# SyncE's requests for x one slot later and behind low-rank inputs and weights; TensorE's register reads behind the first product

## The chip, the cores and the metric

The kernel runs on one core of a Trainium2 chip. The metric is the device time of one execution in microseconds (us). A core has TensorE (PE in the profile, with PEld for its weight loads), VectorE (DVE), ScalarE (ACT), GpSimd (POOL) and SyncE (SP), which here only issues DMAs. Each engine works through its own list of instructions in order; semaphores order them against each other, and an instruction that waits holds all that stands behind it on its engine.

## The reference

The input x has 16 batches of 512 tokens with 512 features. Each batch has its own low-rank factors and condition. `gelu` is exact, the router picks 4 of 16 experts, each with 128 hidden units.

```python
z1 = einsum('bfi,bir->bfr', x, v[:, 0]) / 512
z = einsum('bfr,bor->bfo', z1, u[:, 0]) / 16
c = gelu(einsum('bfi,oi->bfo', x, W) + fc_bias + z + cond)
prob = softmax(c @ w_router + b_router)
mask = the 4 largest of 16 per token
h = relu(einsum('nd,ebd->neb', c, w1b) + b1b)
y = einsum('neb,ebd,ne->nd', h, w2b, mask) + b2
out = x + y
```

## The kernel before

Work runs in slots `s` = 0 to 99, written out by hand in the same order on every engine. In slots 0 to 63 (`SLOTS`) each slot does one piece of 128 tokens of the first layer: batch `b` = s // 4, quarter `q` = s % 4. TensorE's `layer(s)` makes it from a high and a low part of x and W (three products in place of one of full precision), with the low-rank term as one product more; `lowrank_in(b)` (q = 0) makes the factors. ScalarE applies `gelu`, TensorE transposes the result (`turn_batch`) and multiplies it with the router weights (`router`); per batch VectorE chooses experts (`logits`, `choose`, `choose_rest`, `place`) between small products of TensorE (`turn_logits` at the end of a slot with q = 1, `ranks` at q = 2, `counts` at q = 3, `positions` at q = 0). GpSimd's `place_rows(b, q)`, seven slots behind the layer, scatters each row to the lists of its four experts in HBM (`xg`), four indirect DMAs a slot, and `place_tiles` writes the table of tiles (`table`).

From slot 28 (`LAG`) on an expert tile of up to 512 rows is worked on in each slot, j = s - 28, 72 tiles (`NTILE`), so from 28 to 63 both kinds of work are interleaved. In slot s TensorE turns tile j + 1 (`turn_tile`, L1294: two quarters at the slot's start, two later), makes the hidden layer of tile j (`ffn1`, L1310 and L1315) and the result of tile j - 1 (`ffn2`, L1341). ScalarE and VectorE split what TensorE turned into high and low parts (`take_tile`), split the first and second weights of the tile's expert, and copy results out; GpSimd's `send` scatters them to `yt`, four indirect DMAs a slot. From tile 49 on a tile is two halves of 256 rows with an expert each. From tile 48 on (`PRE`) TensorE picks the second weights itself by a register that it loads from the tile's table row (`tabi`, L1289, inside `turn_tile` behind the wait for the tile, two registers for two experts). The last stage, from about 1430 us, sums the four results of each token with x and b2.

SyncE asks for all that comes from HBM, in the order of its own slots. `load_x(s)` (L331) reads a piece of 128 tokens into `stx`, 256 KB, and from piece 6 on waits first for VectorE's split of piece s - 2 (`v_xl` >= s - 1), since two buffers alternate. VectorE and ScalarE split piece s + 4 in slot s (`split_x`). `load_u(b + 1)` and `load_v(b + 2)` (q = 2) read the low-rank factors (`fu`, `fv`); `load_u` waits also for `turn_logits` of the batch before, since the logits share its buffer. Slots 2 to 17 read one expert's weights each (`w1f`, `w2f`, 256 KB each), slots 28 and on, every third, a padding of `xg` (L419). `load_tile(j + 2)` (L371 to L391) waits for the table, for the scattered rows that the tile may hold (L379), for TensorE's turn of tile j (L385), VectorE's ids of it (L386) and its split of the first weights of tile j (L387), and then asks for the rows (L389, 1056 KB) and the table row (L391). TensorE's `turn_tile` of tile j + 2 in slot s + 1 waits for both.

Of the kernel before, what the change touches and what calls it, by code (L numbers as in the profile page):

```python
# [9 lines left out]
NE = 16  # L10
# [7 lines left out]
NTILE = FULL + (HALVES + 1) // 2  # L18
SLOTS = 4 * NB
LAG = 28  # L20
# [10 lines left out]
PRE = 48  # L31
# [26 lines left out]
def chunks(j):  # L58

    return 2 if j == NTILE - 1 and HALVES % 2 == 1 else 4  # L60


def experts(j):

    return 1 if j < FULL else chunks(j) // 2


def x_buffer(s):

    return s if s < 4 else s % 2  # L70
# [53 lines left out]
def home(j):  # L124

    return 0 if j % 2 == 0 else 1 if j < HOME else 2
# [56 lines left out]
def rows_in(j):  # L183

    return sum(16 * (experts(i) + 1) for i in range(j % 2, j + 1, 2))


def per_half(j):

    return sum(experts(i) for i in range(j + 1))  # L190


def adaln_ffn(nc, xT, xrow, fvT, fuT, cond, fc, wT, wrT, br, w1T, b1T, w2T, b2R, outT):
    with ExitStack() as ctx:
        def sb(name, shape, dt):
            return ctx.enter_context(nc.sbuf_tensor(name, shape, dt))
# [56 lines left out]
        tabi = sb("tabi", [P, 2, 2, 4], I32)  # L253
# [73 lines left out]
        def _(sp):  # L327
            def load_x(s):
                if s >= 4:
                    sp.wait_ge(v_xl, s - 3 if s < 6 else s - 1)  # L330
                sp.dma_start(stx[:, x_buffer(s), :], xT[s]).then_inc(s_x[x_buffer(s)], 16)  # L331

            def load_v(b):
                if b > 0:
                    sp.wait_ge(v_v, b)
                sp.dma_start(fv[:, :, :], fvT[b]).then_inc(s_fv, 16)

            def load_u(b):
                if b > 0:
                    sp.wait_ge(v_u, b)  # L340
                if b > 1:
                    sp.wait_ge(p_lt, b - 1)
                sp.dma_start(fu[0:ZP, :], fuT[b]).then_inc(s_fu, 16)
                sp.dma_start(fu[ZP:ZB, :], gbd[b:b + 1, :].broadcast_to([2, D])).then_inc(s_fu, 16)
# [17 lines left out]
            r = [sp.alloc_register(f"r_sp{n}") for n in range(4)]  # L362
# [31 lines left out]
            def load_sum(i):  # L394
                n = len(xin)
                if i >= n:
                    sp.wait_ge(v_sum, 2 * (i - n) + 2)
                sp.dma_start(xin[i % n], xrow[i * SUM:(i + 1) * SUM, :].rearrange(
                    "(p h) d -> p h d", p=P)).then_inc(s_xr[i % n], 16)
# [5 lines left out]
            for s in range(LAG + NTILE):  # L405
                b, q = divmod(s, 4)
                j = s - LAG
                if s + 6 < SLOTS:
                    load_x(s + 6)
                if q == 2 and b + 1 < NB:  # L410
                    load_u(b + 1)
                if q == 2 and b + 2 < NB:
                    load_v(b + 2)
                if 2 <= s < 2 + NE:
                    sp.dma_start(w1f[:, s - 2, :], w1T[s - 2]).then_inc(s_ws, 16)
                    sp.dma_start(w2f[:, s - 2, :], w2T[s - 2]).then_inc(s_ws, 16)
                if LAG <= s < LAG + 3 * NE and (s - LAG) % 3 == 0:
                    e = (s - LAG) // 3
                    sp.dma_start(xg[e * LREG:e * LREG + HALF, :],  # L419
                                 xrow.rearrange("r d -> (r d)")[0:HALF * W].rearrange("(r d) -> r d", d=W)  # L420
                                 ).then_inc(s_pad, 16)
                if 0 <= j + 2 < NTILE:
                    load_tile(j + 2)
                if s == SLOTS + 16:
                    sp.wait_ge(p_tn, TURN_BATCH[SLOTS - 1] + 1)
                    sp.wait_ge(v_ix, NB)
                    sp.wait_ge(v_p2, NE)
                    sp.wait_ge(v_w2, PRE)
                    sp.wait_ge(p_lt, NB)
                    sp.wait_ge(v_u, NB)  # L430
                    sp.dma_start(b2f[:, :], b2R).then_inc(s_b2, 16)
                if SLOTS + 16 <= s < SLOTS + 16 + EARLY:
                    load_sum(s - SLOTS - 16)
# [744 lines left out]
        def _(pe):  # L1178
# [32 lines left out]
            def wait_taken(n):  # L1211

                if n >= 0 and TAKEN[n] is None:
                    pe.wait_ge(a_tn, n + 1)
                elif n >= 0:
                    pe.wait_ge(v_tn, TAKEN[n])
# [11 lines left out]
            def router(s):  # L1228

                b, half = divmod(s // 2, 2)  # L1230
                pe.wait_ge(a_tn, TURN_BATCH[s] + 1)
                if s == 1:
                    pe.wait_ge(s_br, 48)
                if b > 0:
                    pe.wait_ge(v_sv, b)
                if b > 0 and half == 1:
                    pe.wait_ge(v_tb, b)
                for k in range(KC):
                    last = pe.matmul(rps[2 * NE * k:2 * NE * (k + 1), half * 256:(half + 1) * 256], wrz[:, k, :],
                                     gs[:, k, :], start=True, stop=True)  # L1240
                last.then_inc(p_r, 1)
# [38 lines left out]
            r = [pe.alloc_register(f"r_pe{n}") for n in range(6)]  # L1280
            expert = {}

            def turn_tile(j, c):
                if c == 0:
                    pe.wait_ge(s_gr[j % 2], rows_in(j))
                    if j >= PRE:
                        expert[j] = []
                        for h in range(experts(j)):
                            pe.reg_load(r[2 * (j % 3) + h], tabi[0:1, j % 2, h, 0:1])  # L1289
                            expert[j].append(pe.snap(r[2 * (j % 3) + h], min_val=0, max_val=NE - 1))  # L1290
                n = TURN_TILE[j, c]
                wait_taken(n - 2)
                for k in range(KC):
                    last = pe.transpose(trn[n % 2][:, k * P:(k + 1) * P], grs[j][:, c, k * P:(k + 1) * P],  # L1294
                                        idf[:, :])
                last.then_inc(p_tn, 1)

            def ffn1(j):
                pe.wait_ge(v_w1, per_half(j))
                pe.wait_ge(a_tn, TURN_TILE[j, chunks(j) - 1] + 1)  # L1300
                if j > 0:
                    pe.wait_ge(a_hv, per_half(j - 1))
                pe.wait_ge(v_z, min((j + LAG - 1) // 4 + 1, NB))
                g = gsbs[home(j)]
                n = TILE if j < FULL else HALF
                parts = [slice(h * n, (h + 1) * n) for h in range(experts(j))]
                for h, cols in enumerate(parts):
                    for k in range(KC):
                        for a in (HI, LO):
                            pe.matmul(hid[:, cols], w1x[h][:, a, k * P:(k + 1) * P], g[:, k, HI, cols],  # L1310
                                      start=(h == 0 and k == 0 and a == HI), stop=False)
                pe.wait_ge(v_tn, TAKEN[TURN_TILE[j, chunks(j) - 1]])
                for h, cols in enumerate(parts):
                    for k in range(KC):
                        last = pe.matmul(hid[:, cols], w1x[h][:, HI, k * P:(k + 1) * P], g[:, k, LO, cols],  # L1315
                                         start=False, stop=(h == len(parts) - 1 and k == KC - 1))
                last.then_inc(p_f1, 1)
# [48 lines left out]
            for s in range(LAG - 1, SLOTS + 1):  # L1366
                b, q = divmod(s, 4)
                j = s - LAG
# [27 lines left out]
            for s in range(SLOTS + 1, LAG + NTILE + 1):  # L1396
                j = s - LAG
                if j + 1 < NTILE:
                    for c in range(2):
                        turn_tile(j + 1, c)  # L1400
                if s == SLOTS + 1:
                    router(SLOTS - 1)
                if s == SLOTS + 4:
                    positions(NB - 1)
                if s == SLOTS + 6:
                    positions(NB)
                if j < NTILE:
                    ffn1(j)
                if j + 1 < NTILE:
                    for c in range(2, chunks(j + 1)):  # L1410
                        turn_tile(j + 1, c)
                for c in range(chunks(j - 1)):
                    ffn2(j - 1, c)
                if s == SLOTS + 1:
                    turn_logits(NB - 1)
                if s == SLOTS + 2:
                    ranks(NB - 1)
                if s == SLOTS + 3:
                    counts(NB - 1)
# [36 lines left out]
```

## Time and profile before

| | us |
|---|---|
| median of 3 runs | 1648.52 |
| lowest and highest run | 1642.79, 1649.10 |
| the profiled execution | 1648.12 |
| its span, first to last instruction | 1646.3 |
| TensorE busy | 951.5 (58%) |
| VectorE busy | 837.2 (51%) |
| ScalarE busy | 583.9 (35%) |
| GpSimd busy | 576.1 (35%) |
| mean granted clock of TensorE | 0.785 |
| stages: first layer alone, interleaved, tiles alone, sum | 0 to 213, to 1054, to 1420, to 1646 |

The profile gives for each engine when it was busy and what ended its waits: the instruction or DMA whose semaphore update came last. A trailing q (SPq, PEldq) is an engine's sequencer, so a wait or an issue. "issue" is time for which no releaser is seen, "remote" a semaphore update that no recorded instruction matches. A wait is named by the instruction that follows it: "PE trn L1294 <- DMA tabi<-table" is TensorE idle ahead of the tile's first transpose until its table row, asked for last, has landed.

### The profile page before, as it was taken

What the parts mean: (1) busy time and instruction counts of PE and PEld (TensorE: products, weight loads), DVE (VectorE), ACT (ScalarE), POOL (GpSimd) and SP (SyncE); (2) the same over time, 40 slices, a digit from 0 to 9 for tenths busy, and PEclk for the clock granted to TensorE, in tenths of its full rate; (3) what the DMA queues carried; (4) which work ended last, traced back from release to release, by engine and by line L of the source; (5) the groups of instructions that cost most, each with busy time, mean ns of one, the idle gap of its engine ahead of it and who ended that gap; (6) DMA issues with size and microseconds to landing.
All of it is one profiled execution on the core that took longest, in us unless ns stands there. A gap on an engine that the chain in (4) does not pass through costs nothing.

```text
span 1646.3 us, 17908 instructions
## 1 busy us (share of the span) xinstructions
PE 951.5 (58%) x4924; PEld 765.4 (46%) x4924; DVE 837.2 (51%) x1966; ACT 583.9 (35%) x1063; POOL 576.1 (35%) x589
## 2 busy tenths in 40 slices
PE   8755656466556465565565479866888898400000
PEld 7543545355445354454354357654777777300000
DVE  4432333333334242343343346563786786698777
ACT  6332333233233242333333245552665566200000
POOL 0554431332333323243423426556444344400000
PEclk9977787787777777787777789987999999755555
DMA  5765443534543534434434557657668765799999
GB/s 188 257 236 188 147 162 121 177 126 147 170 143 143 170 107 166 162 135 159 167 120 153 176 185 249 237 210 257 223 223 271 263 209 204 273 419 427 425 430 395
DMA packets 103234, 354.82 MB, mean 216 GB/s; under 512 B 29961, under 2 KB 29961, under 8 KB 92384
## 3 DMA queue, kind: packets, MB, share of 16 engines
q1 hardware_dynamic: 59104, 217.21, 38.5%
q0 software_dynamic: 43936, 136.37, 21.2%
q8 instruction: 41, 0.67, 0.2%
q14 instruction: 57, 0.47, 0.1%
q10 hardware_dynamic: 96, 0.10, 0.0%
HBM read 200.47 MB, written 169.65 MB: 225 GB/s over the span
## 4 chain that ended last, share of the span: by engine, by line
PE 39%; DMA 26%; issue 11%; DVE 8%; another core or an unknown queue 6%; SPq 5%; ACT 4%; POOL 1%; ACTq 1%; DVEq 0%; POOLq 0%
DMA tabi<-table 15%; PE hid L1310 9%; PE trn L1294 8%; PE lay L1204 8%; DMA w2l<-yt 8%; PE yps L1341 5%; PE hid L1315 3%; DVE xs L813 2%; PE hid L1190 1%; DVE stx L1026 1%; PE trn L1224 1%; ACT xs L585 1%; DMA outT<-ys 1%; PE lay L1341 1%
## 5 line engine op out<-in xcount | busy, mean ns | idle before, releaser
L547 POOL DMA_INDIRECT yt<-ys,ids x238 | 256.0, 1076 | 450.0 <-ACT ys L690 332.0
L1294 PE MATMUL trn<-idf,gr 128*128 128x128 f32 x720 | 127.8, 334 | 354.8 <-DMA tabi<-table 327.5
L521 POOL DMA_INDIRECT xg<-grow,ix x224 | 219.5, 980 | 231.5 <-DVE ix L909 167.5
L1294 PEld LDWEIGHTS trn<-idf,gr 128*128 128x128 f32 x720 | 105.5, 173 | 373.7 <-DMA tabi<-table 335.6
L1204 PE MATMUL lay<-w2l,xs 128*128 128x512 f32 x768 | 199.6, 411 | 0.0
L1204 PEld LDWEIGHTS lay<-w2l,xs 128*128 128x128 f32 x768 | 147.9, 198 | 31.0
L633 ACT ACTIVATE gsb<-trn 128x512 fp32r<-128x512 f32 x144 | 81.0, 598 | 190.8 <-PE trn L1294 187.5
L844 DVE TENSOR_TENSOR above<-gr,tabi 128x12 f32<-128x12 int32 x45 | 7.6, 169 | 263.5 <-DMA tabi<-table 263.5
L633 ACT ACTIVATE xs<-trn 128x512 fp32r<-128x512 f32 x88 | 50.4, 597 | 211.5 <-PE trn L1294 160.5
L835 DVE TENSOR_TENSOR gsb<-trn,gsb 128x512 fp32r<-128x512 f32 x144 | 94.5, 686 | 55.4 <-ACT gsb L633 48.9
L663 ACT ACTIVATE hv<-hid,b1c 128x512 f32<-128x512 f32 (+1 forms) x94 | 52.7, 584 | 191.2 <-PE hid L1315 159.8
L1010 DVE COPY ys<-yps 128x512 f32<-128x512 f32 x97 | 66.8, 689 | 72.4 <-PE yps L1341 62.2
L813 DVE TENSOR_TENSOR xs<-stx,xs 128x512 fp32r<-128x512 f32 x64 | 44.1, 691 | 101.7 <-ACT xs L585 92.0
L1310 PE MATMUL hid<-gsb,w1c 128*128 128x512 f32 (+1 forms) x288 | 92.2, 478 | 1.7 <-DVE w2c L976 1.7
L835 DVE TENSOR_TENSOR xs<-trn,xs 128x512 fp32r<-128x512 f32 x88 | 58.6, 687 | 53.1 <-ACT xs L633 45.9
L1294 PE MATMUL trn<-idf,grow 128*128 128x128 f32 x424 | 60.6, 282 | 28.8 <-issue 10.8
L1310 PEld LDWEIGHTS hid<-gsb,w1c 128*128 128x128 f32 x288 | 65.9, 259 | 14.1 <-DVE w2c L976 2.4
L547 POOL DMA_INDIRECT yt<-stx,ids x48 | 49.4, 1029 | 56.6 <-ACT stx L690 43.7
L1341 PE MATMUL yps<-w2l 128*128 128x512 f32 x246 | 68.9, 418 | 0.0
L1294 PEld LDWEIGHTS trn<-idf,grow 128*128 128x128 f32 x424 | 47.3, 143 | 43.6 <-issue 26.6
L1310 PE MATMUL hid<-xs,w1c 128*128 128x512 f32 x176 | 67.0, 543 | 0.0
L612 ACT ACTIVATE grow<-lay 128x512 f32<-128x512 f32 x56 | 33.4, 597 | 90.8 <-PE lay L1209 55.4
(220 smaller groups left out, 2026.0 us busy)
## 6 DMA issues: line engine op xcount, KB each, us to landing
gr<-xg SPq DMA_DIRECT2D x45, 1056.0 KB
xs<-yt SPq DMA_DIRECT2D x16, 2048.0 KB, 19.8
w2l<-yt SPq DMA_DIRECT2D x15, 2048.0 KB, 20.2
grow<-xg SPq DMA_DIRECT2D x45, 528.0 KB
stx<-xT SPq DMA_DIRECT2D x64, 256.0 KB, 4.9
outT<-ys SPq DMA_DIRECT2D x31, 512.0 KB, 21.0
xg<-xrow SPq DMA_DIRECT2D x16, 528.0 KB
w2f<-xrow SPq DMA_DIRECT2D x16, 512.0 KB, 14.8
```

Source lines behind the costliest of these rows:

```text
L521: pool.indirect_dma_start(out=xg, out_offset=bass.IndirectOffsetOnAxis(ap=ix[:, row_buffer(b), q, k:k + 1], axis=0), in_=grows[row_buffer( ...
L547: pool.indirect_dma_start(out=yt, out_offset=bass.IndirectOffsetOnAxis(ap=ids[:, j % 8, c:c + 1], axis=0), in_=yss[result_buffer(j)][:, c, ...
L633: act.activation(gsbs[home(j)][:, :, HI, c * P:(c + 1) * P], trn[n % 2][:, :].rearrange("p (k t) -> p k t", k=KC), ACT.Copy).then_inc(a_tn, 1)
L663: act.activation(hv[:, h * n:(h + 1) * n], hid[:, h * n:(h + 1) * n], ACT.Relu, bias=b1c[:, bass.DynSlice(e[h], 1)]).then_inc(a_hv, 1)
L813: dve.tensor_tensor(xs[:, x_home(b), :, LO, cols], stx[:, x_buffer(s), :].rearrange("p (k t) -> p k t", k=KC), xs[:, x_home(b), :, HI, col ...
L835: dve.tensor_tensor(gsbs[home(j)][:, :, LO, c * P:(c + 1) * P], trn[n % 2][:, :].rearrange("p (k t) -> p k t", k=KC), gsbs[home(j)][:, :, ...
L1010: dve.tensor_copy(yss[result_buffer(j)][:, c, :], ypss[result_bank(j, c)][:, :]).then_inc(v_y, 1)
L1204: pe.matmul(lay[s % 2][:, :], xs[:, x_home(b), k, h, cols], wls[:, k, a, :], start=(k == 0 and a == HI and h == HI), stop=False)
L1294: last = pe.transpose(trn[n % 2][:, k * P:(k + 1) * P], grs[j][:, c, k * P:(k + 1) * P], idf[:, :])
L1310: pe.matmul(hid[:, cols], w1x[h][:, a, k * P:(k + 1) * P], g[:, k, HI, cols], start=(h == 0 and k == 0 and a == HI), stop=False)
L1315: last = pe.matmul(hid[:, cols], w1x[h][:, HI, k * P:(k + 1) * P], g[:, k, LO, cols], start=False, stop=(h == len(parts) - 1 and k == KC - 1))
L1341: last = pe.matmul(ypss[result_bank(j, c)][:, :], hx[:, c * P:(c + 1) * P], w[a], start=(i == 0), stop=(i == 2))
```

## The change

In a slot SyncE asks for x behind `load_u`, `load_v` and the weights. In slots 0 to 26 it is still piece s + 6; slot 27 asks for none; from slot 28 to 58 it is piece s + 5. `load_x` and its wait are as before, and so is the place of the padding and of `load_tile` behind it. TensorE's register reads leave `turn_tile` and stand behind `ffn1(j)`, for tile j + 1, without a wait of their own (the wait for the tile was passed at the slot's start).

```diff
             for s in range(LAG + NTILE):
                 b, q = divmod(s, 4)
                 j = s - LAG
-                if s + 6 < SLOTS:
-                    load_x(s + 6)
                 if q == 2 and b + 1 < NB:
                     load_u(b + 1)
...
                     sp.dma_start(w2f[:, s - 2, :], w2T[s - 2]).then_inc(s_ws, 16)
+                if s < LAG - 1:
+                    load_x(s + 6)
+                elif LAG <= s < SLOTS - 5:
+                    load_x(s + 5)
                 if LAG <= s < LAG + 3 * NE and (s - LAG) % 3 == 0:
...
             def turn_tile(j, c):
                 if c == 0:
                     pe.wait_ge(s_gr[j % 2], rows_in(j))
-                    if j >= PRE:
-                        expert[j] = []
-                        for h in range(experts(j)):
-                            pe.reg_load(r[2 * (j % 3) + h], tabi[0:1, j % 2, h, 0:1])
-                            expert[j].append(pe.snap(r[2 * (j % 3) + h], min_val=0, max_val=NE - 1))
...
+            def read_experts(j):
+
+                expert[j] = []
+                for h in range(experts(j)):
+                    pe.reg_load(r[2 * (j % 3) + h], tabi[0:1, j % 2, h, 0:1])
+                    expert[j].append(pe.snap(r[2 * (j % 3) + h], min_val=0, max_val=NE - 1))
...
                 if j < NTILE:
                     ffn1(j)
+                if PRE <= j + 1 < NTILE:
+                    read_experts(j + 1)
```

## Rows read from the trace of the kernel before

**Rows 1.** The page's fourth part: the chain that ended last, by line.

```profile
DMA tabi<-table 15%; PE hid L1310 9%; PE trn L1294 8%; PE lay L1204 8%; DMA w2l<-yt 8%; PE yps L1341 5%; PE hid L1315 3%; DVE xs L813 2%; PE hid L1190 1%; DVE stx L1026 1%; PE trn L1224 1%; ACT xs L585 1%; DMA outT<-ys 1%; PE lay L1341 1%
```

**Rows 2.** Windows: length; PE, PEld, DVE, ACT, POOL busy; clock, DMA share, GB/s.

```profile
42.00:206.00 164.00, 104.12 (x525) 77.50 (x525) 56.61 (x255) 52.65 (x91) 83.41 (x85) 0.80 0.59 207
...
213.00:985.00 772.00, 448.00 (x2102) 358.84 (x2102) 285.66 (x786) 258.46 (x461) 259.32 (x252) 0.76 0.44 151
985.00:1165.00 180.00, 136.11 (x685) 106.35 (x685) 102.57 (x297) 84.91 (x154) 101.31 (x101) 0.88 0.66 234
...
1157.00:1405.00 248.00, 214.62 (x1332) 184.01 (x1331) 184.12 (x401) 153.92 (x301) 113.44 (x110) 0.97 0.71 235
```

**Rows 3.** Waits, 213 to 985 us: us in total, times, longest.

```profile
PE trn L1294 <- DMA tabi<-table: 323.5, 31, 13.0
```

**Rows 4.** SyncE's own waits, 213 to 985 us.

```profile
SPq L331 <- DVE xs L813: 622.5, 29, 25.0
SPq L379 <- DMA xg<-grow,ix: 7.1, 1, 7.1
```

**Rows 5.** The chain that ended last, in order: start, us, what.

```profile
413.56 0.33 SPq L331
...
437.12 0.70 DVE xs L813
...
437.84 0.33 SPq L331
...
439.75 6.70 DMA tabi<-table
...
446.49 1.97 PE trn L1294 x8
```

**Rows 6.** The same chain later: its longest tile landing of the stage.

```profile
939.99 9.73 DMA tabi<-table
```

**Rows 7.** TensorE's timeline: starts of slots 27, 59 and 64.

```profile
213.51 1.97 PE L1294 MATMUL trn<-idf,gr 128*128 128x128 f32 x8 [0.62 <-issue]
...
985.22 1.32 PE L1294 MATMUL trn<-idf,gr 128*128 128x128 f32 x8
...
1053.73 1.04 PE L1294 MATMUL trn<-idf,gr 128*128 128x128 f32 x8
```

**Rows 8.** SyncE's timeline: table row requests of slots 59, 60 and 71.

```profile
981.46 0.43 SPq L391 DMA_DIRECT2D tabi<-table  x1
...
992.96 0.45 SPq L391 DMA_DIRECT2D tabi<-table  x1
...
1157.47 0.42 SPq L391 DMA_DIRECT2D tabi<-table  x1
```

**Rows 9.** Waits of the whole trace whose releaser is unknown.

```profile
DVE fu L863 <- remote: 53.3, 6, 12.0
...
ACT hv L663 <- remote: 26.3, 5, 9.5
```

**Rows 10.** SyncE's timeline in a slot with q = 2 and padding.

```profile
389.27 0.33 SPq L331 DMA_DIRECT2D stx<-xT  x1
...
390.88 0.57 SPq L419 DMA_DIRECT2D xg<-xrow  x1
...
394.18 0.43 SPq L391 DMA_DIRECT2D tabi<-table  x1
```

**Rows 11.** The page's sixth part: x, KB each, us to landing.

```profile
stx<-xT SPq DMA_DIRECT2D x64, 256.0 KB, 4.9
```

**Rows 12.** The chain at the start of slot 82.

```profile
1251.19 8.26 DMA tabi<-table
1259.45 0.92 issue
1260.37 1.94 PE trn L1294 x8
```

**Rows 13.** Waits, 1190 to 1417 us.

```profile
PE trn L1294 <- DMA tabi<-table: 9.9, 5, 2.8
```

## Prediction

> **What bounds the kernel now.** I read the chain that ended last first: 15% of the span is the landing of the tile DMAs, for which TensorE waits in `turn_tile` [rows 1]. The windows by stage show where [rows 2]. Between 213 and 985 us, while batches and expert tiles run interleaved, TensorE is busy 448 of 772 us at a granted clock of 0.76 (a mixture of the levels 1.2 and 2.4 GHz), the DMA engines carry 44%, GpSimd is busy 259 us. No engine is full. From 985 to 1165 us the clock is 0.88 and DMA 66%, from 1157 to 1405 us 0.97 and 71%. The waits of the slow stage: 31 waits of TensorE for the tile, 323.5 us, about 10 us in each slot [rows 3]. Then SyncE's own waits: 622.5 us in 29 waits stand at L331, the wait inside `load_x`, and behind it, of all that `load_tile` itself waits for, the largest is 7.1 us, once [rows 4].
>
> The chain through one slot tells why [rows 5]. VectorE splits piece s + 4 of x at 437.12; only then may SyncE ask for piece s + 6 (437.84), and behind that, in the same queue, for tile j + 2 (439.75). Its rows land 6.70 us later, TensorE starts the slot at 446.49, and the split of the next piece stands near the end of that slot's VectorE work. So each slot holds a closed loop: split, x request, tile request, landing, whole slot, split. From x request to x request (413.56 to 437.84) it is 24.3 us. A tile needs of this only what its own waits in `load_tile` say: tile j turned, its ids taken, its first weights split, all of the slot before, and the scattered rows.
>
> **The change part by part.**
>
> *x one slot later (slots 28 to 58).* SyncE now asks in slot s for piece s + 5, whose wait is for the split of piece s + 3, made in the slot before. No request is added or dropped (31 in this stage). The loop of rows 5 stays but spans two slots instead of one: with this landing 24.3 / 2 = 12.2 us a slot, and with the longest landing of the chain, 9.73 us [rows 6], (24.3 + 3.0) / 2 = 13.7 us. That is a floor, no longer the bound, if a slot's other work is as long.
>
> What a slot costs with the tiles there in time is shown by the trace itself: from slot 58 on SyncE has no x to ask for. TensorE starts slot 27 at 213.51, slot 59 at 985.22 and slot 64 at 1053.73 [rows 7]. So the 32 slots that are held take 771.7 us, 24.1 each; the five free slots with the same layer, turns, feed-forward and scatters take 68.5, 13.7 each. Over the twelve free slots by SyncE's tile requests (981.46 to 1157.47) it is 176.0 us, 14.67 each [rows 8]. These have less TensorE work towards their end, but they also hold stalls whose releaser the profile does not know: one of ScalarE's waits for the hidden layer is 9.5 us long, and VectorE's waits for the router product come to 53.3 us in six, up to 12.0 [rows 9]. The held slots have besides a split of x on ScalarE and VectorE and 256 KB of DMA that slots 60 to 63 lack; both engines are busy at most 57% of the free stage [rows 2], so I put no own term for it, and take the larger row, 14.67. 32 x 14.67 = 469; the saving is 771.7 - 469 = 302 us. Ends for this term: 12.2 a slot (390, saving 381) and 17.7 (below; 566, saving 205).
>
> *What the request is moved behind.* In every fourth slot `load_u` (two DMAs) and `load_v` (one) now come first, and `load_u` waits for TensorE's `turn_logits`, the last work of the slot before: the queue holds x and the tile behind it until then. In such a slot x, u, v and a third of the time the padding are issued from 389.27 to 390.88, and the tile's last request is at 394.18, 4.9 us behind the first one [rows 10]. From the slot's start: 4.9 + 6.7 = 11.6, with the long landing 14.6, against a free slot of 14.7. It fits, barely; if it misses, it costs up to 1 us in 8 slots, inside the rounding of the term above. An x piece lands after 4.9 us [rows 11] (seen where it could be timed) and is needed by ScalarE at the end of the next slot, some 20 us behind the request: no cost. In slots 2 to 17 the two weight requests go ahead of x. x still waits there for the same split of its own slot, which is later than the weights' issue, and is needed two slots on: 0, with -5 to +10 us as ends, since the early stage has DMA at 59% and stalls too [rows 2, 9]. The padding write (every third slot) stays ahead of the tile as before.
>
> *Registers (slots 75 to 98).* Before, TensorE's two loads stand between the landing of a tile and its first transpose: landing 8.26 us, then 0.92 us of issue, then the turn [rows 12]. Behind ffn1 they go beside matmuls that are queued already. Where the tile is late 0.92 us goes; where it is not, queued matmuls cover the loads today too. Five of TensorE's gaps there are put down to the tile [rows 13]; I take seven of the 24 slots, since the loads themselves hide a landing that is just late: 6 us. Ends: 24 x 0.92 = 22 us gained in every slot, or 22 us lost, if the second pair of turns starts later by the loads and nothing covers that. What is late next in those slots is the landing itself, through the split of the first weights.
>
> **Sum.** The profiled execution took 1648.1 us (span 1646.3 and 1.8 around it), the median of the runs is 1648.5, so no correction. 1648.1 - 302 - 6 = 1340 us. After slot 59 I leave all else as it is: the last stage of 216 us is not touched.
>
> **A rule against it.** GpSimd's instructions take 259.3 / 252 = 1.03 us each in the held stage and 101.3 / 101 = 1.00 us in the free one, where VectorE's busy share is 0.57 instead of 0.37 [rows 2]: denser VectorE work did not slow them. The Trainium skill ("SBUF — State Buffer", section "Who interferes with whom") says that the port pair shared by GpSimd and VectorE is an exclusive lock, so that one waits for the other's whole instruction, and with the change more of both overlap. By that rule the time would be the one of the last rival below; the trace so far does not agree.
>
> **Rivals.**
> - *The two-slot loop is the bound* and the free work is shorter than in slots 59 to 70, because more TensorE work runs at full clock: 12.2 a slot, 390 us, total 1648 - 381 - 6 = 1261 us. For it: one free slot is 11.5 us long by SyncE's requests (981.46 to 992.96 [rows 8]). Against: five of them together take 13.7 each.
> - *Late completions in each batch.* With GpSimd at 8 indirect DMAs a slot (10.6 us with gaps of 0.3) in a slot of 14, its streaks get longer, and each batch of four slots pays one stall of VectorE's longest, 12.0 us [rows 9]: 14.67 + 3.0 = 17.7 a slot, 566 us, total 1648 - 205 - 6 = 1437 us. For it: six such waits in 16 batches now, with GpSimd less busy for most of them. Against: the five free slots take 13.7 each with their stalls.
> - *The scatter's landing takes the place of x* in every fourth slot (7.1 us where it was seen once [rows 4]): 8 x 7.1 = 57 us, total 1397 us. Slots of two lengths would show it.
> - *Slower than before: a stall of that size in every slot*, in ScalarE's and VectorE's waits on TensorE, from the faster mixture of scatters, tile reads and x. 13.7 + 12.0 = 25.7 a slot, 822 us, total 1648 + 50 = 1698 us. It decides from 24.1 - 13.7 = 10.4 us a slot on. Six waits averaging 8.9 us in the whole trace are far from one in each slot.
> - *It does not do what it says*: another wait of `load_tile` is satisfied just as late as x's, and the start stays: 1648 us. Those waits are all for the slot before, so there is little for it.
> - *GpSimd becomes the bound*: if each of its instructions doubled, 8 x (2.06 + 0.30) = 18.9 a slot, 604 us, total 1648 - 168 - 6 = 1474 us. The rows of GpSimd speak against it.
>
> **How the numbers follow.** The forecast of 1340 (1295 to 1385) 0.57; the two-slot loop 0.14; late completions per batch 0.14; the scatter's landing 0.08; GpSimd as bound 0.02; does nothing 0.02; slower 0.03. The range runs from 1272, between forecast and the short rival (its outer half left out), to 1430, just short of the batch stalls; about 2 in 10 is left out. Less than 0.5%, 8 us, can't be told from no change here. Faster by more: all but two cases, 0.95; within: 0.02; slower: 0.03.
>
> **What would show it.** Right: SyncE's wait at L331's place falls from 622 us to under half, TensorE's wait for tabi from 323 to under 50, the start of slots 28 to 58 14 to 15 us apart, granted clock there above 0.9, DMA above 65%; in the last tile slots no 0.9 us of issue between landing and turn. Wrong: slots of 17 us and more with ScalarE's and VectorE's waits put down to no known releaser; a wait at `load_u` or for scattered rows in every fourth slot that TensorE then repeats; or an early stage longer than 206 us.

## The result and the profile after

The changed kernel takes 1355.8 us, median of 4 runs (1348.3 to 1366.9), beside 1645.7 us of the kernel before in its 4 runs (1641.3 to 1649.1): a ratio of 0.8245, with a 95% interval of 0.8171 to 0.8320. The forecast was 1340, the range 1272 to 1430. The profiled execution took 1362.6 us, its span is 1360.8.

The windows of the changed kernel, by stage. Columns as in [rows 2]. The bounds are the starts of TensorE's first transpose in slots 27, 59, 75 and 98 (98 is the last slot that turns a tile).

```profile
0.00:200.70 200.70, 148.07 (x754) 110.67 (x754) 78.77 (x330) 79.96 (x137) 88.82 (x116) 0.85 0.63 215
200.70:684.77 484.07, 412.62 (x2117) 323.35 (x2117) 281.61 (x789) 254.77 (x461) 254.01 (x253) 0.93 0.71 240
684.77:906.40 221.63, 169.75 (x808) 132.96 (x809) 126.25 (x342) 107.27 (x193) 116.48 (x116) 0.87 0.63 224
906.40:1119.00 212.60, 184.54 (x1173) 156.10 (x1172) 154.26 (x333) 128.88 (x257) 94.42 (x92) 0.99 0.70 231
1119.00:1360.80 241.80, 13.33 (x75) 10.53 (x73) 191.25 (x175) 8.70 (x18) 15.90 (x14) 0.54 0.96 399
```

The second row answers the interleaved row of [rows 2]: the same work (TensorE 2117 records, 2102 in the slightly shorter window before) in 484 instead of 774 us, the granted clock 0.93 instead of 0.76, DMA 71% instead of 44%. TensorE's busy time fell from 448 to 413 us although its work is the same, since more of it ran at the upper of the two levels, 2.4 GHz.

SyncE's own waits in this stage, 201 to 685 us (us in total, times, longest), answering [rows 4]:

```profile
SPq L331 <- DVE xs L815: 219.9, 18, 15.6
SPq L342 <- PE rps L1250: 77.7, 7, 12.0
SPq L379 <- DMA xg<-grow,ix: 1.7, 1, 1.7
```

And the waits of the other engines in the same window, the tile's row answering [rows 3] and the five largest without a known releaser answering [rows 9]:

```profile
ACT xs L635 <- remote: 36.0, 12, 5.0
ACT grow L614 <- remote: 29.8, 8, 4.9
ACT hv L665 <- remote: 19.0, 5, 6.0
DVE fu L865 <- remote: 18.1, 6, 4.4
DVE ys L1012 <- remote: 14.7, 4, 4.9
PE trn L1291 <- DMA tabi<-table: 13.9, 8, 3.5
```

The wait inside `load_x` went from 622 to 220 us, and TensorE's wait for the tile from 323.5 us in 31 waits to 13.9 in 8: the tile is there. SyncE now waits at L342 too, inside `load_u`. New in bulk are the waits put down to "remote", which the last two sections come back to.

To see where the time went in every kernel, I took the same four starts from each trace's TensorE timeline. A stage is the difference of two of them:

| span, us | to slot 27 | slots 27-58 (each) | 59-74 | 75-97 | rest | span |
|---|---|---|---|---|---|---|
| before | 211.4 | 773.8 (24.2) | 208.6 | 211.9 | 240.6 | 1646.3 |
| after | 200.7 | 484.1 (15.1) | 221.6 | 212.6 | 241.8 | 1360.8 |
| difference | -10.7 | -289.7 | +13.0 | +0.7 | +1.2 | -285.5 |

The first start of slot 27 before is at 211.44, one half-turn ahead of the row at 213.51 that [rows 7] has. The stage so far called 771.7 us is 773.8 by that.

### The profile page after: what moved, and what is told of

It is laid out like the page before. It is cut to its first block, busy times and chain, and to the rows that moved or that the text cites. A ratio compares the mean times of both kernels' runs of the same rounds, so it can differ in the third digit from the quotient of the medians.

```text
span 1360.8 us, 17932 instructions
## 1 busy us (share of the span) xinstructions
PE 928.3 (68%) x4924; PEld 733.6 (54%) x4924; DVE 832.1 (61%) x1966; ACT 579.6 (43%) x1063; POOL 569.6 (42%) x589
## 4 chain that ended last, share of the span: by engine, by line
PE 35%; DMA 18%; DVE 13%; issue 12%; another core or an unknown queue 9%; ACT 6%; POOL 3%; SPq 2%; ACTq 1%; DVEq 0%; POOLq 0%
DMA w2l<-yt 10%; PE hid L1314 7%; PE trn L1291 7%; PE lay L1206 6%; PE yps L1345 5%; DMA tabi<-table 5%; PE hid L1319 4%; PE hid L1192 2%; DVE stx L1028 2%; POOL xg L523 2%; DMA yt<-ys,ids 2%; DMA outT<-ys 1%; POOL yt L549 1%; PE lay L1345 1%
## 5 line engine op out<-in xcount | busy, mean ns | idle before, releaser
L549 POOL DMA_INDIRECT yt<-ys,ids x238 | 243.6, 1023 | 302.9 <-ACT ys L692 172.2
L523 POOL DMA_INDIRECT xg<-grow,ix x224 | 223.1, 996 | 150.3 <-DVE ix L911 86.3
L1206 PE MATMUL lay<-w2l,xs 128*128 128x512 f32 x768 | 204.7, 419 | 0.0
L1206 PEld LDWEIGHTS lay<-w2l,xs 128*128 128x128 f32 x768 | 152.1, 203 | 32.9
L1291 PE MATMUL trn<-idf,gr 128*128 128x128 f32 x720 | 109.8, 295 | 68.2 <-ACT stx L623 15.7
L1291 PEld LDWEIGHTS trn<-idf,gr 128*128 128x128 f32 x720 | 89.6, 152 | 86.7 <-issue 26.0
L1314 PE MATMUL hid<-gsb,w1c 128*128 128x512 f32 (+1 forms) x288 | 78.9, 424 | 2.9 <-DVE w2c L978 2.9
L1314 PEld LDWEIGHTS hid<-gsb,w1c 128*128 128x128 f32 x288 | 56.1, 222 | 13.6 <-DVE w2c L978 4.0
L1345 PE MATMUL yps<-w2c,hh 128*128 128x512 f32 x180 | 60.9, 420 | 1.6 <-ACT stx L692 1.6
L692 ACT ACTIVATE ys<-yps 128x512 f32<-128x512 f32 x97 | 57.8, 596 | 9.4 <-remote 4.7
```

The costliest lines, as they stand in the source:

```text
L523: pool.indirect_dma_start(out=xg, out_offset=bass.IndirectOffsetOnAxis(ap=ix[:, row_buffer(b), q, k:k + 1], axis=0), in_=grows[row_buffer( ...
L549: pool.indirect_dma_start(out=yt, out_offset=bass.IndirectOffsetOnAxis(ap=ids[:, j % 8, c:c + 1], axis=0), in_=yss[result_buffer(j)][:, c, ...
L692: act.activation(yss[result_buffer(j)][:, c, :], ypss[result_bank(j, c)][:, :], ACT.Copy).then_inc(a_y, 1)
L1206: pe.matmul(lay[s % 2][:, :], xs[:, x_home(b), k, h, cols], wls[:, k, a, :], start=(k == 0 and a == HI and h == HI), stop=False)
L1345: last = pe.matmul(ypss[result_bank(j, c)][:, :], hx[:, c * P:(c + 1) * P], w[a], start=(i == 0), stop=(i == 2))
```

## The experiments

They ran on three chips, in two groups of times, and this has to be known ahead of them. On chip 7 the kernel before took 1646.2 us (median of 7 runs, 1638.6 to 1653.2), as on the chip of the result above (1645.7), whose number is not on record. On chip 1 the same program took 1536.9 us (19 runs, 1527.3 to 1543.3), on chip 6 1536.8 (13 runs, 1527.7 to 1545.1). I write A for chip 7 and the chip of the result, and B for chips 1 and 6: the names stand for the two groups of times, not for two chips. The changed kernel itself ran on A alone. The four runs from x_only to order_only in the table are of chip 1, the four below them of chip 6. Ratios are always to the kernel before on the same chip; traces of the kernel before exist for A alone. In the columns, a slot of 27-58 is the mean of 32, and the others are whole stages.

| run | chip | median us | ratio, 95% interval | to slot 27 | slot 27-58 | 59-74 | 75-97 |
|---|---|---|---|---|---|---|---|
| changed_again | A | 1357.2 | 0.8233 (0.8176 to 0.8290) | 201.6 | 15.15 | 217.3 | 212.2 |
| tile_first | A | 1345.7 | 0.8187 (0.8161 to 0.8213) | 196.9 | 14.69 | 216.7 | 211.8 |
| x_behind_tile | A | 1351.9 | 0.8227 (0.8197 to 0.8256) | 197.6 | 14.96 | 220.0 | 212.1 |
| gpsimd_pauses | A | 1284.6 | 0.7798 (0.7766 to 0.7830) | 198.3 | 13.58 | 204.0 | 210.8 |
| x_only | B | 1186.2 | 0.7704 (0.7668 to 0.7741) | 149.1 | 13.19 | 175.0 | 202.4 |
| registers_only | B | 1530.0 | 0.9959 (0.9931 to 0.9987) | 149.3 | 24.26 | 171.9 | 195.9 |
| later_only | B | 1178.6 | 0.7658 (0.7630 to 0.7686) | 150.9 | 12.93 | 174.4 | 205.6 |
| order_only | B | 1532.3 | 0.9969 (0.9946 to 0.9992) | 147.8 | 24.04 | 173.9 | 202.1 |
| short_pauses | B | 1179.8 | 0.7697 (0.7652 to 0.7742) | 149.0 | 13.05 | 173.9 | 197.0 |
| pauses_everywhere | B | 1209.5 | 0.7875 (0.7829 to 0.7921) | 153.7 | 13.36 | 190.5 | 196.1 |
| pauses_tile_first | B | 1205.5 | 0.7858 (0.7815 to 0.7902) | 153.5 | 13.07 | 191.2 | 196.7 |
| before_with_pauses | B | 1535.1 | 0.9989 (0.9959 to 1.0020) | 146.1 | 23.77 | 182.0 | 203.3 |

**The two halves of the change: x_only and registers_only.** The first is the kernel before with only SyncE's part of the diff, the second with only TensorE's:

```diff
 x_only, SyncE
-                if s + 6 < SLOTS:
-                    load_x(s + 6)
...
+                if s < LAG - 1:
+                    load_x(s + 6)
+                elif LAG <= s < SLOTS - 5:
+                    load_x(s + 5)
 registers_only, TensorE
-                    if j >= PRE:
-                        expert[j] = []
...
+                if PRE <= j + 1 < NTILE:
+                    read_experts(j + 1)
```

> SyncE's part of the change alone; TensorE's register reads stay in the turn as in the kernel before. My theory: it carries all of the gain, and the register part nothing, since in the changed kernel's trace the gap of about 1 us has only moved from ahead of the turn to behind ffn1: within 5 us of the changed kernel's 1356 us. Rival (the registers brought the 6 us of the sum): 6 us more than the changed kernel.

> TensorE's part alone; SyncE as in the kernel before. My theory: within 3 us of the kernel before (1646 us), with slots 75 to 98 taking 211 to 213 us as in both kernels. Rival (0.92 us in seven slots): 6 us less than before. Rival (a bubble in each of 23 slots): up to 20 us more.

x_only has the large gain, registers_only leaves the held stage at 24.26 us a slot. What the register reads are worth shows in the last tile slots: 202.4 us with the reads in the turn, 195.9 with them behind `ffn1`. Both expectations held the registers for nothing; on B the rival, 6 us, came in (6.9 us between the two medians, ratio 0.9959, so the size is known to some 4 us). The chain that ended last in x_only, as [rows 12] of before, still has the gap between landing and turn; in registers_only it hasn't. Columns: start, us, what; first x_only, then registers_only.

```profile
839.87 7.86 DMA tabi<-table
847.73 0.93 issue
848.66 1.06 PE trn L1296 x8
```

```profile
1178.86 8.05 DMA tabi<-table
1186.91 0.04 issue
1186.96 1.08 PE trn L1289 x4
```

**Later or behind: later_only and order_only.** The change does two things to the request for x. Each alone, on the kernel before:

```diff
 later_only: at its old place, ahead of load_u
-                if s + 6 < SLOTS:
+                if s < LAG - 1:
                     load_x(s + 6)
+                elif LAG <= s < SLOTS - 5:
+                    load_x(s + 5)
 order_only: behind load_u, load_v and the weights
-                if s + 6 < SLOTS:
-                    load_x(s + 6)
...
+                if s + 6 < SLOTS:
+                    load_x(s + 6)
```

> Kernel before, but x is asked one slot later from slot 28 on and stays ahead of the low-rank inputs and weights in every slot. My theory: the loop over two slots is the whole effect, so slots 27 to 58 take about 15 us each, and only the early stage keeps its 211 us instead of 201 us: 1356 + 10 = 1366 us. Rival (the order counts as well in slots with q = 2): the load_u wait no longer holds x, 1350 us. Rival (the order carries the gain): near 1640 us.

> Kernel before, but each slot's x request (still piece s + 6) stands behind low-rank inputs and weights. My theory: x still waits for the split of its own slot, so slots 27 to 58 stay at 24 us each; the early stage gains 10 us because weights leave the queue earlier: 1636 us. Rival: the early 10 us are another effect or chance: 1646 us.

later_only keeps the whole gain (0.7658 beside x_only's 0.7704, intervals that overlap), order_only has a slot of 24.04 us and gains some 5 us in all (0.9969, an interval that nearly reaches 1); the 10 us that were expected of it in the early stage did not come (147.8 us beside 149.3 in registers_only). So the gain is that of the slot later, and the new place among the low-rank inputs has no part in it on B. The windows of both stages, later_only first:

```profile
150.90:564.80 413.90, 386.40 (x2117) 309.16 (x2117) 282.32 (x791) 257.20 (x465) 259.50 (x258) 0.97 0.83 284
```

```profile
147.80:917.20 769.40, 446.29 (x2117) 357.59 (x2117) 286.28 (x789) 259.11 (x462) 267.58 (x258) 0.77 0.45 154
```

**The change once more: changed_again.** No edit, on chip 7 beside the next three.

> The changed kernel itself, beside the experiments. The four kernels of the first group ran at 0.93 of the earlier time of the kernel before (1537 instead of 1646 us) and showed no late completion of TensorE at all, where the first traces show 70 and 178. My theory: that lateness depends on the chip and not on the kernel; where it is absent, x part and register part add up: 1186 - 6 = 1180 us, ratio 0.767. Where it is present: 1356 us, ratio 0.824. Rival: the register part is lost beside the x part: 1186 us.

1357.2 us and 15.15 us a slot: the first trace's 15.13 was no accident. The stages agree to 1 us each but for slots 59 to 74, 217.3 and 221.6, so a single trace's number there is good to about 4 us. The early stage is no better: four kernels with the same early slots have it at 196.9 to 201.6 us on A.

**The wait at load_u: tile_first.** In the changed kernel, from slot 28 on, the tile is asked for first, then u, v, x and the padding.

```diff
+                if 0 <= j + 2 < NTILE:
+                    load_tile(j + 2)
+                if q == 2 and s >= LAG and b + 1 < NB:
+                    load_u(b + 1)
+                if q == 2 and s >= LAG and b + 2 < NB:
+                    load_v(b + 2)
+                if LAG <= s < SLOTS - 5:
+                    load_x(s + 5)
...
-                if 0 <= j + 2 < NTILE:
-                    load_tile(j + 2)
```

It was made for this place in the changed kernel's chain, in a slot with q = 2 and padding (L342 is `load_u`'s wait for `turn_logits`):

```profile
482.73 1.90 PE rps L1250 x8
...
484.64 0.02 SPq L342
...
486.31 1.58 SPq L421
...
491.92 1.39 SPq L387
...
494.05 0.70 SPq L389
...
494.77 7.32 DMA tabi<-table
502.09 0.04 issue
502.13 1.39 PE trn L1291 x8
```

From L342 to the table's request SyncE needs 10.1 us (484.64 to 494.77), with u, v, x, the padding (1.58 us alone) and the steps of `load_tile` in one row, and the landing is 7.32 more: 17.5 us for a slot that should be 15. This is the longest of the eight such slots of the stage: from `load_u`'s first request to the tile's last the three with padding take 7.2, 10.1 and 9.5 us, the five without 3.4 to 4.7. In x_only on B the same rows take 4.4 to 4.6 and 3.4 to 3.6 us; why they are longer on A is open.

> Changed kernel, but from slot 28 on the tile request stands first in SyncE's slot, then u, v, x, padding; nothing of the x chain or of load_u's wait is left ahead of the tile. My theory: the two-slot loop and load_u's wait still cost the interleaved stage: TensorE's waits for the tile (20, 48 us in x_only) go, slots fall from 13.2 to the 12.0 us of the free slots, 30 to 38 us less than the changed kernel. Rival (those waits hide others, TensorE's own work and its partners are the bound): less than 8 us.

14.69 us a slot on A, 1345.7 beside 1357.2 us of the change: 11.5 us less, where 30 to 38 were expected and under 8 by the rival. In the traces the held stage is 14.6 us shorter, but so is the early stage by 4.7, which the edit leaves alone. The two ratios' intervals touch (0.8176 to 0.8290 and 0.8161 to 0.8213), so the sign is likely and the size is not settled.

**x not later but behind the tile: x_behind_tile.** The kernel before, with the request for piece s + 6 moved to the end of the slot.

```diff
-                if s + 6 < SLOTS:
-                    load_x(s + 6)
...
                 if 0 <= j + 2 < NTILE:
                     load_tile(j + 2)
+                if s + 6 < SLOTS:
+                    load_x(s + 6)
```

> Kernel before with one move: in each slot load_x(s + 6), which still waits for the split of its own slot, stands behind load_tile(j + 2) instead of ahead of everything. x is not asked later in slots. My theory: what counts is only which wait the tile stands behind; the tile now waits for the x chain of the slot before, as in later_only: ratio 0.766 (or 0.82 where completions are late). Rival (asking for x later is itself what helps, by less DMA traffic or a later split): near 1.0.

It asks for the same piece as the kernel before, in the same slot, and waits for the same split. It is not independent of later_only, though: from slot 28 on both kernels send SyncE's requests in the same order, tile j + 2, then piece s + 6, then the next slot's u, v, padding and tile j + 3; only the slot under which the program writes the piece differs. So it repeats later_only on A. SyncE's waits in the held stage, as [rows 4], of this run and then of later_only:

```profile
SPq L331 <- DVE xs L813: 292.2, 27, 14.2
SPq L379 <- DMA xg<-grow,ix: 2.5, 1, 2.5
```

```profile
SPq L331 <- DVE xs L815: 294.1, 31, 13.8
```

292 us of waiting at L331, more than in the changed kernel, and yet 14.96 us a slot and 1351.9 us in all; 294 us in later_only, which has the shortest slots of all, 12.93 us. How long SyncE waits for a split is no measure of the cost. What cost 290 us was that tile j + 2 stood behind piece s + 6 instead of ahead of it, and that piece waits for a split that is made only in the present slot.

**GpSimd's streaks: gpsimd_pauses.** The changed kernel, with five small memsets, each waiting for the one before, ahead of and behind the four scatters to `xg` in slots 31 to 66. They compute nothing that is used.

```diff
+            def pause():
+                for _ in range(5):
+                    if paused[0]:
+                        pool.wait_ge(g_p, paused[0])
+                    paused[0] += 1
+                    pool.memset(idle[:, :], 0.0).then_inc(g_p, 1)
...
                 if 0 <= s - 7 < SLOTS and not first:
+                    pause()
                     place_rows((s - 7) // 4, (s - 7) % 4)
+                    pause()
```

> Changed kernel, with GpSimd made to pause (five small chained memsets, an estimated 1 to 2 us) ahead of and behind the four scatters of a slot in slots 31 to 66, so that no more than six indirect DMAs stand back to back. My theory where completions are late: the lateness needs a streak of about eight, so it shrinks, and the kernel is 10 to 40 us faster than the changed one in spite of the pauses. Where they are not late: 0 to 25 us slower. Rival (the lateness comes from DMA traffic, not from GpSimd's streaks): it stays with the pauses.

1284.6 us: work was added to an engine, and 72.6 us went (1357.2 to 1284.6), on chip 7, where 10 to 40 were expected. GpSimd's timeline in one slot (start, us, engine, line, operation, then the idle time before it):

```profile
322.56 0.82 POOL L563 MEMSET idle<- 128x16 f32 x5
323.54 0.97 POOL L525 DMA_INDIRECT xg<-grow,ix  x1 [0.15 <-issue]
324.81 0.96 POOL L525 DMA_INDIRECT xg<-grow,ix  x1 [0.30 <-issue]
326.08 0.96 POOL L525 DMA_INDIRECT xg<-grow,ix  x1 [0.30 <-issue]
327.35 0.96 POOL L525 DMA_INDIRECT xg<-grow,ix  x1 [0.31 <-issue]
328.31 0.80 POOL L563 MEMSET idle<- 128x16 f32 x5
```

The window of the held stage, beside the changed kernel's second row above:

```profile
198.27:632.80 434.53, 392.49 (x2115) 312.48 (x2116) 281.19 (x789) 258.00 (x464) 285.31 (x524) 0.96 0.77 266
```

Against changed_again the held stage is 50.1 us shorter (484.7 to 434.6) and slots 59 to 74 are 13.3 us shorter. The stages that the edit leaves alone differ by 3.3 us (to slot 27) and 1.4 us (75 to 97). This kernel is the fastest of all that ran on A.

**What in the pause does it: short_pauses, pauses_everywhere, pauses_tile_first, before_with_pauses.** One memset in place of five; five behind every group of indirect DMAs in all slots; the same with the order of tile_first; and the pauses of gpsimd_pauses in the kernel before.

```diff
 short_pauses
-                for _ in range(5):
+                for _ in range(1):
 pauses_everywhere
                 if 0 <= s - 7 < SLOTS and first:
                     place_rows((s - 7) // 4, (s - 7) % 4)
+                    pause()
                 if 0 <= j < NTILE:
                     for c in range(chunks(j)):
                         send(j, c)
+                    pause()
                 if 0 <= s - 7 < SLOTS and not first:
                     place_rows((s - 7) // 4, (s - 7) % 4)
+                    pause()
```

> Changed kernel with the pauses of gpsimd_pauses cut to one memset of 16 columns each (0.1 to 0.2 us of work instead of 0.8). If any other instruction between two groups of four indirect DMAs is what ends the lateness: about 1285 us, as gpsimd_pauses. If the time of the pause is what counts: between, 1320 to 1357 us. On a chip without late completions: within 5 us of the changed kernel (1180 us).

> Changed kernel with a pause of five memsets behind each group of four sends or four scatters in every slot, the early stage's and the last slots' too. Theory (streaks make the lateness): the early stage falls from about 200 to 170 us and slots 59 to 74 from 204 us (gpsimd_pauses) to about 190, total 1240 to 1265 us. Rival (the early stage is held by DMA traffic): early stage stays near 200 us or grows by the pauses' 14 us.

> pauses_everywhere with the tile request first in SyncE's slot. With completions less late, slots are shorter and the tile comes late more often (25 waits, 47 us in gpsimd_pauses), so the order should bring more than the 11 us it brought in tile_first: 20 to 35 us less than pauses_everywhere. Rival (those waits cover others): under 10 us.

> Kernel before with the pauses of gpsimd_pauses. There GpSimd has streaks of six at most in the interleaved stage and completions are late only outside it. Theory: slots 27 to 58 stay at 24.2 us, and only the slots behind 58 gain, as in gpsimd_pauses (217 to 204 us): 1630 to 1646 us. Rival (the pauses help by something else in each slot, such as fewer transfers at a time): 40 to 70 us less, as in the changed kernel.

These four ran on chip 6, and there was nothing there for them to mend: none of the eight traces of B has a wait put down to "remote". So they tell what pauses cost, and nothing of why they help on A. What the changed kernel would take on B I estimate from two runs of chip 1: x_only's 1186.2 less the 6.3 us that registers_only gained (its ratio of 0.9959 on 1536.9) is 1179.9. short_pauses took 1179.8, so a single memset at each place costs nothing that shows. pauses_everywhere took 1209.5, a loss of some 30 us, of which the stages show 17 in slots 59 to 74 (190.5 beside short_pauses' 173.9), 10 in slots 27 to 58 and 5 ahead of them. In the kernel before the pauses come to nothing in all (0.9989, an interval around 1); beside the other two kernels with held slots on B, slots 59 to 74 are 8 to 10 us longer (182.0 beside 173.9 and 171.9) and the held stage 9 to 16 us shorter (23.77 us a slot beside 24.04 and 24.26). Whether its forecast for a chip with late completions was right is open.

pauses_tile_first against pauses_everywhere was a miss: 4 us (1209.5 to 1205.5), not the 20 to 35 that I had set. SyncE's waits in its slots 27 to 58 say why:

```profile
SPq L381 <- DMA xg<-grow,ix: 102.4, 15, 12.2
SPq L387 <- PE trn L1309: 78.9, 18, 7.6
SPq L333 <- DVE xs L833: 51.2, 11, 5.5
```

Without the tile request behind `load_u`, it stands at its own conditions: the scattered rows (L381) and TensorE's turn of tile j (L387). An earlier place in the queue gains only up to the next wait.

## Why the prediction was right, step by step

**What bounds the kernel.** Right: each slot held a closed loop through SyncE's queue. later_only on B and x_behind_tile on A let the tile's request out ahead of the piece's and both have the whole gain; order_only leaves it behind the piece and has none. The signs set for it came in: the wait at L331 under half (220 of 622 us), TensorE's wait for the tile under 50 us (13.9), the clock above 0.9 (0.93), DMA above 65% (71%). The slots' starts are 15.13 us apart, just outside the 14 to 15 that were set. Of the signs against it one showed in part: a wait at `load_u` in seven of eight slots with q = 2 (77.7 us), of which little came through to TensorE. Another could not tell anything: "an early stage longer than 206 us" holds for the kernel before already, with 211.4. The Trainium skill ("DMA: Bandwidth & Descriptors", section "Rules for kernel authors") advises to issue a DMA early and wait for it late. For the x piece alone that speaks against the change; by the runs, an early request whose wait is not yet fulfilled costs what stands behind it in the queue, 9 us in each of 32 slots here (24.18 to 15.13).

**The size of the held slot.** 14.67 us was taken, 15.13 measured: 289.7 us saved instead of 302. Near, but the value holds two things that the prediction did not take apart. The twelve free slots behind 14.67 contained late completions, and so do the slots of the changed kernel. B, where no wait has an unknown releaser, shows the slot without them: 12.93 (later_only) to 13.19 (x_only). On B the five free slots of registers_only take 12.0 each (925.6 to 985.5), against the 13.7 of [rows 7] on A. So the number was right because a stalled row was used to forecast stalled slots. The 12.2 to 13.7 of the two-slot loop lie about the slots of B, but what bounds these is not shown: TensorE still has 14 waits for the tile there in later_only, 34.5 us in all.

**The sum.** 1340 beside 1355.8 us is nearer than the terms are. In the traces the held stage saved 12 us less than forecast, the last tile slots 7 less, and slots 59 to 74, put at nothing, lost 13.0; the early stage, put at nothing too, gained 10.7, and the median of the runs lies 6.8 us under the profiled execution (1362.6). The last two made up for over half of the others by luck.

**The rival of late completions.** Half right. They did become more with denser work. Counting, in the records, semaphore updates of TensorE that come over 1.5 us behind the end of the last matmul that raises the same semaphore, there are 70 in the trace of before and 180 after (the expectations have 178). In the 32 held slots it is 4 before and 99 after; 36 of the 70 fell in slots 59 to 74, which hold the row that the forecast was taken from. But a slot lost some 2 us to them (15.1 beside about 13 on B, a comparison between chips), not 3 on top of 14.67, and gpsimd_pauses got 1.57 back on A itself. Slots 59 to 74, which the prediction left alone, paid 13.0 us in the first trace and 8.7 in the second.

**`load_u` ahead of the tile.** "It fits, barely" was too kind for slots with padding: SyncE's own time there is 7.2 to 10.1 us on A where 4.9 was taken, while the landing of 7.32 is within what was taken. The queue also starts only when `turn_logits` of the slot before is done (77.7 us of waits at L342, in seven slots). The 11.5 us between changed_again and tile_first, with the reserve named above, are the price of all that stands ahead of the tile, u, v, x and padding together, where 8 had been allowed for u and v; the share of `load_u` alone was not tried.

**The early stage.** 0 was taken, with -5 to +10 as ends: 10.7 and 9.8 us shorter on A (211.4 to 200.7 and 201.6), outside the ends on the good side. All five traces on A in which x goes later in the slot are 10 to 15 us shorter than the single one of before. On B there is no such gain: order_only 147.8 beside 149.3 and 146.1 in two kernels with the old order. It was seen on A alone; how it comes about was not tried.

**The registers.** 6 us were expected. On B that is what they are: the last tile slots take 195.9, 197.0, 196.1 and 196.7 us in the four kernels with the reads behind `ffn1`, and 202.4, 205.6, 202.1 and 203.3 in the four without, 6.9 us between the means. On A nothing shows: 212.6, 212.2, 211.8 and 210.8 with, 211.9 and 212.1 without. The changed kernel's chain on A shows both sides of it:

```profile
973.13 9.63 DMA tabi<-table
982.80 1.09 PE trn L1291 x8
...
994.68 0.96 PE hid L1319 x8
995.64 0.98 issue
996.62 1.25 PE trn L1291 x8
```

Landing and turn now touch, as forecast. But in another slot the gap of about 1 us stands behind `ffn1` (L1319), ahead of the second half of the turns: "queued matmuls cover the loads" holds only where something is queued. That is the mechanism of the upper bound, a loss. Whether it is what takes the gain on A, or late completions do, no run tells.

**GpSimd.** It did not become the bound: 254.01 us in 253 instructions, 1.00 us each, with VectorE busy 58% of the time (281.6 of 484.1) instead of 37%. The Trainium skill ("SBUF — State Buffer", section "Who interferes with whom") limits the lock on the shared port pair to VectorE instructions in a two-port mode, and to those with two SBUF inputs against a GpSimd instruction that reads SBUF. How many of VectorE's instructions here are of such a kind was not counted; by their mean, 1.03 us before and 1.00 after, GpSimd's were not made longer.

## What to carry to other kernels

Where one queue issues for several users, list for each request which wait it stands behind, not only its own: a request that may wait for the present slot's work belongs behind those that need only the slot before, or one slot later. Read the size of what is left from a stretch of the same trace in which the suspected loop is absent, and look which stalls that stretch itself contains. And a gain in a stage that was held by one loop uncovers what the loop had hidden: the same program differs by 109 us between A and B, and in its 32 held slots by nothing that shows (24.18 us each on A, 24.26 in registers_only on B), so the change saved 290 us on A, and its SyncE half alone 351 on B (1536.9 to 1186.2).

## What the chips showed beside this

On A, TensorE's completions come late while GpSimd issues indirect DMAs back to back. An example from the changed kernel's early stage; GpSimd's timeline first, the middle of 17 indirect DMAs left out:

```profile
104.17 1.15 POOL L523 DMA_INDIRECT xg<-ys,ix  x1 [3.88 <-DVE ix L911]
...
123.75 0.96 POOL L523 DMA_INDIRECT xg<-ys,ix  x1 [0.30 <-issue]
125.01 0.96 POOL L523 DMA_INDIRECT xg<-ys,ix  x1 [0.30 <-issue]
```

TensorE's timeline, then ScalarE's, which takes what TensorE made:

```profile
114.87 0.66 PE L1226 MATMUL trn<-idf,grow 128*128 128x128 f32 x4
123.86 1.89 PE L1250 MATMUL rps<-sumk,fu 128*128 128x16 f32 x8 [8.34 <-issue]
```

```profile
118.16 0.60 ACT L614 ACTIVATE grow<-lay 128x512 f32<-128x512 f32 x1 [5.37 <-remote]
128.67 0.60 ACT L623 ACTIVATE stx<-trn 128x512 f32<-128x512 f32 x1 [9.91 <-remote]
```

The transposes of L1226 ended at 115.5 by the record, and ScalarE's instruction, for which ScalarE had been idle 9.91 us, started at 128.67, 2.7 us behind the end of GpSimd's streak at 125.97. Of the 180 late completions 124 fall in, or just behind, a streak of eight or more, and 78 of these between 1 and 2 us behind its last instruction, stretches that make up 35 of the 1360 us. 56 do not, so streaks are not all of it. No such lateness is seen in what ScalarE or VectorE complete. On B the same stage has longer streaks still (one of 93 in x_only), and there ScalarE waits at most 0.6 us at L623. The row of its waits up to 149 us (us in total, times, longest):

```profile
ACT stx L623 <- PE trn L1226: 6.3, 12, 0.6
```

That the streaks have to do with it on A is supported by one intervention, the pauses, which cut the late completions to 118 and the time by 73 us. What in the pause does it (its time, or that another kind of instruction comes between), what on A makes the completions late, and whether the effect comes with the chip or with something that held for it during these runs, is open: the runs that could tell the first of these apart are of B, where the effect is absent. The Trainium skill ("SBUF — State Buffer", section "Who interferes with whom") names the port pair of VectorE and GpSimd as the single cause of contention and gives TensorE no share in it. The trace of A shows TensorE's completions delayed beside GpSimd by up to 13 us, whatever carries the delay.
